# Fused state-space, attention and feed-forward layer: normalized rows turned by DMA, image mask added by VectorE, leaner sine tables

## The chip, the cores and the metric

The kernel runs on one core of one Trainium2 chip. The metric is the device time of one execution in microseconds (us): median 3081.81 us of three runs (3081.46 to 3085.93). The core has TensorE (PE), VectorE (DVE), ScalarE (ACT), GpSimd (POOL) and SyncE (SP, which issues DMAs), and each engine works through its own instructions in order.

## The reference

The program computes three things in a row, for a batch of 32 images.

1. **State-space rows.** `K = einsum('chn,hnl->chl', Wc, exp(P))` with `P = dt*Lambda*pos`: complex exponentials over 1024 positions for 128 rows of each image, of which the real part is kept. The result (32 x 128 x 1024) gets 77 text rows under each image, so `h` is 32 x 205 x 1024.
2. **Attention with a residual.** `x = layernorm(h)`, `q = x @ wq` (32 heads of 32), `k` and `v` with 8 heads, causal mask, softmax, `out @ wo`, `h = h + out`.
3. **A feed-forward product with a residual.** `h = h + layernorm(h) @ W.T + b`, where `W` is a base matrix plus a low-rank update passed through a Fourier matrix.

```
scores = einsum('bihd,bjhd->bhij', q, k) * SCALE
scores = where(tril(ones((s, s))), scores, finfo.min)
attn = softmax(scores, axis=-1)
```

Precision comes from splitting: each fp32 value is written as a high and a low fp16 part, and a product is three fp16 matmuls (high x high, high x low, low x high).

## The kernel before

Five stages follow one another, each a block that all engines leave together.

**State-space tables and product (`ssm`).** The exponential of a position is a product of a coarse and a fine factor. DVE, ACT and POOL first make four tables `tab[:, 0..3]` of 128 x 2048 (two coarse, two fine: a sine and a quarter-turned sine each) and two tables of magnitudes `size`. The argument of a sine is `f*step` (`bases`, L276), plus a phase by ACT (`turned`, L212), less its nearest whole number by DVE (L297, L298); then ACT takes the sine (L223). `size` is a product on POOL (L186) and an exponential on ACT (L216). POOL multiplies two tables by `size` (L191), DVE the other two (L347). Then 16 chunks of 8 channels run: DVE makes `es` from the tables (two instructions at L356, and L358, which adds the two halves for `SUMMED` = 2 channels so that those need one matmul and not two), POOL multiplies the weights (L199, L200), DVE adds (L362), PE multiplies (L379), ACT copies out (L237).

**Weight split (`prep_qkv`).** Untouched by the change.

**Attention.** This is a software pipeline over images that runs through the *rounds* b = -3 to 32 (`steps`). In round b four images are in work: image b gets softmax and `attn @ v` (`has["att"]`), image b+1 its row maxima (`has["max"]`), image b+2 its projections (`has["qkv"]`), image b+3 its layer norm (`has["ln"]`), and image b+4 is loaded. A round has eight *beats* g = 0 to 7 (`SLOTS`), one for each key head. The order inside a beat is written out by hand for each engine:

- PE: `scores` k = 0 and 1 (L867), `score_rows` k = 0 and 1 (the first image rows, L910 and L912, then text rows), the first half (`FRONT`) of the beat's projection `q` (L930 to L932), `scores` k = 2 (L870), `score_rows` k = 2, the second half, then `weigh` of the beat before (L897), then the other *units* of the beat.
- ACT: three exponentials (L720), three casts to fp16 `ph` (L727), then the high part of each unit (L735, or L733 for maxima).
- DVE: row maxima (L805) k = 0 and 1, a unit's low part left from the beat before, maxima k = 2, low part `pl` (L833), a piece of the layer norm in beats 0 to 3 (last piece L786: subtract the mean, multiply by the inverse deviation, 128 x 1024 and 77 x 1024), `norm` (L754 to L760: divide by the softmax sum), then the low part (L813) of every unit of the beat but the last.
- SP: regrouping copies `restack` (L593, 12 DMAs for each half of `q` or `k`), the maxima rows (L640, L641), the load of image b+4 (L644, L645) and the store of a finished image (L649, L650).

A unit is one result in one of the two PSUM buffers `psJ`: `q` 0 to 7 (one a beat), `v` 0 and 1 (beats 0, 1), `k` 0 and 1 (beats 2, 3), `m` 1 (beat 0) and `m` 0 (beat 4), which are the maxima turned to rows, and `x` 0 to 3 (beats 4 to 7), which are the normalized rows of image b+3 turned to columns by PE (L954) for the projections of the next round. PE starts unit number N of a round only when the low parts of the units 0 to N-2 are done (`wait(pe, pj_lo, base + (n + which - 1))` in `project`).

PE also adds the causal mask: in `score_rows` a matmul of an identity by the mask (L910, 128 x 512 for the image rows) starts the sum in PSUM, and the four score matmuls add to it. DVE's maximum over 512 columns then is one instruction for four heads.

**Output weights (`prep_out`) and output stage (`output`).** Untouched. The output stage already turns its fp16 rows with transposing DMAs (L1215, L1217, L1222, L1224).

Of the kernel before, what the change touches and what calls it, by code (L numbers as in the profile page):

```python
# [16 lines left out]
P = 128  # L17
# [17 lines left out]
SUMMED = 2  # L35
HC = 8
MROW = 32768.0
STACK = 3 * HD
# [32 lines left out]
def ssm(nc, x, txt, log_dt, lam, hcat, ahead, peak):  # L71

    NCH = H // HC
    with ExitStack() as ctx:
# [10 lines left out]
        phase = sb("phase", [P, 4])  # L87
# [38 lines left out]
        ab_ok, base_ok, turned_ok, frac_ok, sine_ok = (sem("ab_ok"), sem("base_ok"), sem("turned_ok"),  # L126
                                                       sem("frac_ok"), sem("sine_ok"))
        size_arg, size_ok, tab_cd, tab_ab = sem("size_arg"), sem("size_ok"), sem("tab_cd"), sem("tab_ab")
# [28 lines left out]
        def _(sp):  # L157
# [6 lines left out]
            sp.wait_ge(tab_ab, 2)  # L164
            sp.wait_ge(tab_cd, 2)
# [11 lines left out]
        def _(pool):  # L177
# [6 lines left out]
            pool.wait_ge(ab_ok, 1)  # L184
            for k in range(2):
                pool.tensor_tensor(size[:, k], per_row(a[:]), per_step(iqr[:, k, :]), ALU.mult).then_inc(size_arg, 1)  # L186

            pool.wait_ge(size_ok, 1)
            for t in range(2):
                pool.wait_ge(sine_ok, t + 1)  # L190
                pool.tensor_tensor(tab[:, t], tab[:, t], size[:, 0], ALU.mult).then_inc(tab_ab, 1)  # L191
# [3 lines left out]
            pool.wait_ge(frac_ok, 4)  # L195
# [7 lines left out]
        def _(act):  # L203
            act.wait_ge(in_small, 48)
            act.activation(dt[:], ldt[:], ACT.Exp).then_inc(dt_ok, 1)

            act.wait_ge(args_ok, 1)
            act.activation(ex[:], args[:, 0].rearrange("p k h -> p (k h)"), ACT.Exp).then_inc(waves_ok, 1)
            act.activation(th[:], args[:, 0].rearrange("p k h -> p (k h)"), ACT.Tanh, scale=0.5).then_inc(waves_ok, 1)
            for t in range(4):  # L210
                act.wait_ge(base_ok, t // 2 + 1)
                act.activation(turned[:, t], bases[t // 2], ACT.Identity, bias=phase[:, t:t + 1]).then_inc(turned_ok, 1)  # L212
            act.wait_ge(la_ok, 1)
            act.activation(ela[:], fla[:, 0], ACT.Exp).then_inc(la_exp_ok, 1)
            act.wait_ge(size_arg, 2)
            act.activation(size, size, ACT.Exp).then_inc(size_ok, 1)  # L216

            act.activation(trig[:], turns[:], ACT.Sin, scale=TWO_PI).then_inc(waves_ok, 1)
            act.wait_ge(la_ok, 2)
            act.activation(tla[:], wla[:], ACT.Sin, scale=TWO_PI).then_inc(la_sin_ok, 1)  # L220
            for t in range(4):
                act.wait_ge(frac_ok, t + 1)
                act.activation(tab[:, t], turned[:, t], ACT.Sin, scale=TWO_PI).then_inc(sine_ok, 1)  # L223

            def factors(ch):

                if ch >= 2:
                    act.wait_ge(e_ok, ch - 1)
                act.copy(ab[ch % 2][:], tab[:, 0:2, ch * HC:(ch + 1) * HC, :]).then_inc(ab_in, 1)
# [11 lines left out]
            act.wait_ge(tab_ab, 2)  # L241
# [9 lines left out]
        def _(dve):  # L251
            chain = Chain(dve, dve_c)

            for t, (top, bottom) in enumerate(((0.25, 0.25), (0.5, 0.0), (0.25, 0.0), (0.0, 0.25))):
                dve.memset(phase[0:N, t:t + 1], top)
                m = dve.memset(phase[N:P, t:t + 1], bottom)
# [18 lines left out]
            for k in range(2):  # L275
                dve.tensor_tensor(bases[k], per_row(f[:]), per_step(iqr[:, k, :]), ALU.mult).then_inc(base_ok, 1)  # L276
# [9 lines left out]
            chain(dve.tensor_tensor(turns[:], turns[:], whole[:], ALU.subtract))  # L286

            v = ila[:].unsqueeze(2).broadcast_to([P, LA, H])
            dve.tensor_tensor(fla[:, 0], a[:].unsqueeze(1).broadcast_to([P, LA, H]), v, ALU.mult).then_inc(la_ok, 1)
# [5 lines left out]
            for t in range(4):  # L295
# [155 lines left out]
def attention(nc, ahead, hcat, acat, qh, ql, kh, kl, escale):  # L451
# [5 lines left out]
    with ExitStack() as ctx:  # L457
# [45 lines left out]
        def units(has):  # L503

            out = []
            for s in SLOTS:
# [7 lines left out]
                if s >= 4 and has["ln"]:  # L514
                    row.append(("x", s - 4))
# [906 lines left out]
```

## Time and profile before

| | us |
|---|---|
| median of three runs | 3081.81 |
| the profiled execution | 3082.04 |
| its span, first to last instruction | 3080.3 |
| state-space stage | 0 to 190.7 |
| weight split, then constants | 190.7 to 246.4 |
| attention | 246.4 to about 1895 |
| output weights | about 1895 to 1996 |
| output stage | 1996 to 3080 |

The profile gives each engine's busy time, the granted clock of PE as a share of full speed, groups of instructions with their mean duration, and for idle time the instruction that ended it. The duration of a pipelined instruction is longer than the distance between two of its kind, so durations may overlap in the timeline.

### The profile page before, as it was taken

Reading aid. Unit: us, or ns where it says so; the run is one execution under the profiler, and the core shown is the slowest. Engines: PE = TensorE matmul, PEld = TensorE weight load, DVE = VectorE, ACT = ScalarE, POOL = GpSimd, SP = SyncE. Lnnn points to the kernel's source line nnn. Section 1 sums busy time; section 2 is a strip of 40 time slices with the busy share of each in tenths; the row PEclk is TensorE's granted clock in tenths of the full one; section 3 lists DMA queues with packets and bytes.
Section 4 is the critical chain, followed back from the end, with each engine's and each line's share of the span. In section 5 each row is a group of like instructions: output and inputs, shape, how many; then the busy total and the mean of one; then the engine's idle time right before and its main releaser. Section 6 shows DMA issues by size and latency. Waiting matters only on the chain. (4 is left out here: it accounts for less than half of the span.)

```text
span 3080.3 us, 70678 instructions
## 1 busy us (share of the span) xinstructions
PE 2781.2 (90%) x27970; PEld 2030.8 (66%) x28224; DVE 1997.8 (65%) x4642; ACT 1094.1 (36%) x2362; POOL 1029.9 (33%) x1402
## 2 busy tenths in 40 slices
PE   0847799999999999999999986699999999999999
PEld 0736698989899898989898883244444444444444
DVE  8874577787787878777787865444444444444443
ACT  3331355555555555555555565211001101100110
POOL 4631254544545454554445454011101110110110
PEclk9977899999999999999999996599999999999999
DMA  5642422222222322222222223154554455455453
GB/s 179 194 116 69 103 58 78 58 75 78 57 76 60 80 58 77 69 65 77 56 76 58 69 49 144 55 122 120 129 137 123 121 133 132 118 127 137 124 122 86
DMA packets 446040, 297.32 MB, mean 97 GB/s; under 512 B 389416, under 2 KB 407976, under 8 KB 445232
## 3 DMA queue, kind: packets, MB, share of 16 engines
q1 hardware_dynamic: 445472, 282.69, 35.7%
q10 hardware_dynamic: 240, 10.09, 1.1%
q8 instruction: 226, 3.70, 0.5%
q14 instruction: 102, 0.84, 0.1%
HBM read 116.36 MB, written 80.61 MB: 64 GB/s over the span
## 5 line engine op out<-in xcount | busy, mean ns | idle before, releaser
L693 POOL TENSOR_SCALAR_AFFINE_SELECT p<-p 128x256 f32<-128x256 f32 (+1 forms) x768 | 334.3, 437 | 762.0 <-ACT p L720 743.6
L805 DVE TENSOR_REDUCE mx<-psS 77x2 f32<-77x410 f32 (+1 forms) x768 | 449.3, 613 | 181.9 <-PE psS L912 110.7
L930 PE MATMUL psJ<-xth,qh 128*128 128x205 f16 x2048 | 522.0, 255 | 24.9 <-DVE qsl L813 24.7
L932 PE MATMUL psJ<-xth,ql 128*128 128x205 f16 x2048 | 518.4, 253 | 0.0
L931 PE MATMUL psJ<-xtl,qh 128*128 128x205 f16 x2048 | 516.5, 252 | 0.0
L720 ACT ACTIVATE p<-psT,escale 128x410 f32<-128x410 f32 (+1 forms) x768 | 410.4, 570 | 276.2 <-PE psT L870 256.8
L698 POOL TENSOR_TENSOR pl<-p,ph 128x410 f16<-128x410 f32 (+1 forms) x512 | 447.7, 894 | 102.5 <-ACT ph L727 95.7
L1257 POOL TENSOR_TENSOR hb<-h,bias_sb 128x1024 f32<-128x1024 f32 x52 | 122.5, 2355 | 962.4 <-DVE h L1293 962.4
L1271 ACT CAST xh<-xn 128x1024 f16<-128x1024 f32 x52 | 54.4, 1045 | 967.1 <-DVE xn L1302 967.1
L1332 PE MATMUL ps5O<-woh,ath 128*128 128x512 f16 x832 | 316.2, 380 | 26.3 <-DMA atl<-al 26.3
L1293 DVE SCALAR_TENSOR_TENSOR h<-ps5O,osc,h_in 128x512 f32<-128x512 f32 x104 | 78.1, 751 | 402.4 <-PE ps5O L1334 402.4
L727 ACT CAST ph<-p 128x410 f16<-128x410 f32 (+1 forms) x768 | 334.3, 500 | 6.6 <-POOL p L693 6.4
L1332 PE MATMUL ps5F<-wfh,xth 128*128 128x512 f16 x832 | 315.4, 379 | 1.2 <-DMA xtl<-xl 1.2
L1334 PE MATMUL ps5O<-woh,atl 128*128 128x512 f16 x832 | 316.2, 380 | 0.0
L1333 PE MATMUL ps5O<-wol,ath 128*128 128x512 f16 x832 | 316.2, 380 | 0.0
L1333 PE MATMUL ps5F<-wfl,xth 128*128 128x512 f16 x832 | 315.5, 379 | 0.0
L1334 PE MATMUL ps5F<-wfh,xtl 128*128 128x512 f16 x832 | 315.5, 379 | 0.0
L897 PE MATMUL psO<-vh,ph 128*128 128x33 f16 (+1 forms) x3072 | 261.4, 178 | 6.9 <-issue 5.1
L897 PE MATMUL psO<-vh,pl 128*128 128x33 f16 (+1 forms) x3072 | 260.4, 178 | 0.0
L897 PE MATMUL psO<-vl,ph 128*128 128x33 f16 (+1 forms) x3072 | 260.4, 178 | 0.0
L897 PEld LDWEIGHTS psO<-vh,ph 128*128 128x128 f16 (+1 forms) x3072 | 245.2, 97 | 9.8 <-issue 9.5
L897 PEld LDWEIGHTS psO<-vl,ph 128*128 128x128 f16 (+1 forms) x3072 | 240.7, 97 | 0.0
(227 smaller groups left out, 5906.9 us busy)
## 6 DMA issues: line engine op xcount, KB each, us to landing
a_in<-acat SPq DMA_DIRECT2D x52, 512.0 KB, 3.8
h_in<-hcat SPq DMA_DIRECT2D x52, 512.0 KB, 4.7
qst<-qsh SPq DMA_DIRECT2D x512, 51.2 KB, 2.1
out<-y SPq DMA_DIRECT2D x51, 512.0 KB, 3.1
hcat<-ob SPq DMA_DIRECT2D x64, 256.0 KB, 4.0
xin<-hcat SPq DMA_DIRECT2D x32, 512.0 KB
acat<-ao SPq DMA_DIRECT2D x32, 512.0 KB
qst<-qsl SPq DMA_DIRECT2D x256, 51.2 KB, 2.1
```

What stands on the lines that cost most here:

```text
L693: pool.affine_select(out=v, in_=v, compare_op=ALU.is_ge, fill=0.0, base=0, pattern=[[0, v.shape[1]], [1, w]], channel_multiplier=-1).then_ ...
L698: pool.tensor_tensor(view(pl, g % 2, k), view(p32, g % 2, k), view(ph, g % 2, k), ALU.subtract).then_inc(lo_pool, 1)
L720: act.activation(view(p32, g % 2, k), ps_view(psT[(g + k) % 2], k), ACT.Exp, scale=(escale[:, 0:1] if k < 2 else escale[0:TXT, 0:1])).then ...
L727: act.copy(view(ph, g % 2, k), view(p32, g % 2, k)).then_inc(hi_done, 1)
L805: dve.tensor_reduce(dst, v, AX.X, ALU.max).then_inc(s_read, 1)
L897: m = pe.matmul(o[:, t, r, :], p, v[0:T[j], j, g, :], start=n == 0, stop=n == len(list_) - 1)
L930: pe.matmul(ps[:, 0:S], wh[:, k, c], xth[:, par, k, :], start=k == 0, stop=False)
L931: pe.matmul(ps[:, 0:S], wh[:, k, c], xtl[:, par, k, :], start=False, stop=False)
L932: m = pe.matmul(ps[:, 0:S], wl[:, k, c], xth[:, par, k, :], start=False, stop=k == KC - 1)
L1332: pe.matmul(ps[h][:], th[:, k, :], wh[:, k, c], start=k == 0, stop=False)
L1333: pe.matmul(ps[h][:], th[:, k, :], wl[:, k, c], start=False, stop=False)
L1334: m = pe.matmul(ps[h][:], tl[:, k, :], wh[:, k, c], start=False, stop=k == KC - 1)
```

## The change

Three parts, in `ssm` and `attention`.

**The normalized rows.** The `x` units, L954 and L786 go. DVE makes the negated mean only (`nmean`); ACT, after the units of beats 4 and 5, subtracts the mean in place and casts the scaled row to fp16 (`high_part`); DVE makes the low part after its `pl` of the same beats (`low_part`), and SP turns four pieces with `dma_start_transpose`, the text rows padded to 80. PE waits for them at the start of the next round. The load and the store of an image move from SP to ACT (load and half a store ahead of beat 2, the other half ahead of beat 6), and on SP the first `k` half now goes ahead of the first `q` half. `norm` has one reciprocal and one product instead of two of each.

**The mask.** L910 goes. For the image rows, DVE adds the mask and takes the maximum with one `tensor_tensor_reduce` a head, four where one reduction stood.

**The tables.** ACT makes `size` and `ela` with 36 exponentials of 128 columns, whose scale is the step. Two rounded arguments are made, not four; the quarter-turned sines come from an absolute value. DVE multiplies all four tables by `size`. `SUMMED` goes, and PE makes two matmuls for each channel.

```
+            for k in range(2):
+                for r in range(LR):
+                    m = act.activation(size[:, k, :, r], a[:], ACT.Exp, scale=iqr[:, k, r:r + 1])
+                m.then_inc(size_ok, 1)
...
+            act.activation(turned[:, 1], turned[:, 0], ACT.Abs, scale=-1.0, bias=phase[:, 0:1]).then_inc(far_ok, 1)
+            act.activation(tab[:, 1], turned[:, 0], ACT.Sin, scale=-TWO_PI, bias=lag[:, 0:1]).then_inc(sine_ok, 1)
+            act.wait_ge(far_ok, 1)
+            act.activation(tab[:, 0], turned[:, 1], ACT.Sin, scale=-TWO_PI, bias=quarter[:, 0:1]).then_inc(sine_ok, 1)
...
-            for t in range(4):
-                dve.wait_ge(turned_ok, t + 1)
-                chain(dve.tensor_scalar(tab[:, t], turned[:, t], ROUND, ROUND, ALU.add, ALU.subtract))
-                dve.tensor_tensor(turned[:, t], turned[:, t], tab[:, t], ALU.subtract).then_inc(frac_ok, 1)
+            chain(dve.tensor_scalar(tab[:, 0], base, phase[:, 0:1], ROUND, ALU.add, ALU.add))
+            dve.scalar_tensor_tensor(turned[:, 0], tab[:, 0], ROUND, base, ALU.subtract,
+                                     ALU.subtract).then_inc(frac_ok, 1)
...
+            for t in range(4):
+                dve.tensor_tensor(tab[:, t], tab[:, t], size[:, t // 2], ALU.mult).then_inc(tab_ok, 1)
...
-                if s >= 4 and has["ln"]:
-                    row.append(("x", s - 4))
...
+                if has["ln"]:
+
+                    wait(sp, pj_filled, base)
+                    for t in range(2):
+                        turn(t, nxt, b + 3)
...
+            def turn(t, to, n):
+                r, cols = ((P, slice(0, P)), (TROWS, slice(P, P + TROWS)))[t]
+                sp.wait_ge(x_hi, 2 * n + t + 1)
+                sp.dma_start_transpose(out=xth[:, to, :, cols], in_=xfh[0:r, t, :]).then_inc(xt_in[to], 16)
+                sp.wait_ge(x_lo, 2 * n + t + 1)
+                sp.dma_start_transpose(out=xtl[:, to, :, cols], in_=xfl[0:r, t, :]).then_inc(xt_in[to], 16)
...
+            def high_part(b, par, t):
+                r, x = T[t], xin[0:T[t], 1 - par, t, :]
+                if t == 0:
+                    act.wait_ge(ln_done, b + 4)
...
+                act.activation(x, x, ACT.Identity, bias=nmean[0:r, t:t + 1]).then_inc(centred, 1)
+                act.wait_ge(centred, 2 * (b + 3) + t + 1)
+                act.activation(xfh[0:r, t, :], x, ACT.Copy, scale=rs[0:r, 3, t:t + 1]).then_inc(x_hi, 1)
...
+                    if g == 2 and has["load"]:
+                        wait(act, x_lo, 2 * (b + 3))
+                        load(b + 4, par)
+                    if g == 2 and has["last"]:
+                        store(b - 1, 1)
+                    if g == 6 and has["att"]:
+                        store(b, 0)
...
+                    if g in (4, 5) and has["ln"]:
+                        high_part(b, par, g - 4)
...
+            def low_part(b, par, t):
+                r = T[t]
+                dve.wait_ge(x_hi, 2 * (b + 3) + t + 1)
+                dve.scalar_tensor_tensor(xfl[0:r, t, :], xin[0:r, 1 - par, t, :], rs[0:r, 3, t:t + 1], xfh[0:r, t, :],
+                                         ALU.mult, ALU.subtract).then_inc(x_lo, 1)
...
+                        for r in range(REP):
+                            m = dve.tensor_tensor_reduce(seen[:, r, :], src[:, r * P:(r + 1) * P], mask[:, 0, :], 1.0, LEAST,
+                                                         ALU.add, ALU.max, mx[:, 0, 4 * j + r:4 * j + r + 1])
+                        m.then_inc(s_read, 1)
...
+                    if has["ln"] and g in (4, 5):
+                        low_part(b, par, g - 4)
...
-                    pe.matmul(ps[:], ident_bf[:], mask[:], start=True, stop=False, skip_group_check=True)
...
+                if has["qkv"]:
+                    pe.wait_ge(xt_in[par], 64 * ((b + 2) // 2 + 1))
```

The order of DVE's instructions before, from `pl` of beat 4 to the maxima of beat 5 (`qsl` here is the low part of q4, `xtl` that of unit x0, `ml` that of m0):

```order
L833 TENSOR_TENSOR pl<-p,ph 128x410 [waits hi_done]
L754 RECIPROCAL rden<-psO 128x4 [waits norm_done,av_done]
L755 RECIPROCAL rden<-psO 77x4
L760 TENSOR_TENSOR ao<-psO,rden 128x128 [waits rec_done]
L760 TENSOR_TENSOR ao<-psO,rden 77x128
L813 TENSOR_TENSOR qsl<-psJ,qsh 128x205 [waits pj_hi]
L813 TENSOR_TENSOR xtl<-psJ,xth 128x4x128 [waits pj_hi]
L805 TENSOR_REDUCE mx<-psS 128x4 [waits s_filled]
L805 TENSOR_REDUCE mx<-psS 77x2 [waits s_filled]
```

The same place on DVE now (`xfl` is the low part of the normalized rows; each `tensor_tensor_reduce` stands as two rows named ISA; the first of four pairs is shown):

```order
L865 TENSOR_TENSOR pl<-p,ph 128x410 [waits hi_done]
L814 SCALAR_TENSOR_TENSOR xfl<-xin,rs,xfh 128x1024 [waits x_hi3]
L784 RECIPROCAL rden<-psO 128x8 [waits norm_done,av_done]
L787 TENSOR_TENSOR ao<-psO,rden 128x2x128 [waits rec_done]
L845 TENSOR_TENSOR qsl<-psJ,qsh 128x205 [waits pj_hi]
L831 ISA seen,mx<-psS,mask 128x128 [waits s_filled]
L831 ISA mx 128x1
```

The wait for `x_hi3` now stands ahead of `norm` and of the low part of q4, and the reduction over 512 columns has become eight instructions.

ACT before, from the last cast of beat 4 to the exponentials of beat 6 (`xth` are the high parts of x0 and x1, `mh` that of m0, `p` are the exponentials):

```order
L727 CAST ph<-p 77x308 [waits masked]
L735 CAST qsh<-psJ 128x205 [waits q_in1,pj_filled]
L735 CAST xth<-psJ 128x4x128 [waits pj_filled]
L733 ACTIVATE mh<-psJ 16x205 [waits m_in0,pj_filled]
L720 ACTIVATE p<-psT,escale 128x410 [waits lo_done,st_filled]
L720 ACTIVATE p<-psT,escale 128x410 [waits lo_pool,st_filled]
L720 ACTIVATE p<-psT,escale 77x308 [waits lo_pool,st_filled]
L727 CAST ph<-p 128x410 [waits masked,av_done]
L727 CAST ph<-p 128x410 [waits masked]
```

ACT now, from the last cast of beat 4 to the store ahead of beat 6 (`xfh` is the high part of the normalized rows):

```order
L754 CAST ph<-p 77x308 [waits masked]
L762 CAST qsh<-psJ 128x205 [waits q_in1,pj_filled]
L760 ACTIVATE mh<-psJ 16x205 [waits m_in0,pj_filled]
L719 ACTIVATE xin<-xin,nmean 128x1024 [waits xt_in3_0,ln_done]
L721 ACTIVATE xfh<-xin,rs 128x1024 [waits centred]
L747 ACTIVATE p<-psT,escale 128x410 [waits lo_done,st_filled]
L747 ACTIVATE p<-psT,escale 128x410 [waits lo_pool,st_filled]
L747 ACTIVATE p<-psT,escale 77x308 [waits lo_pool,st_filled]
L754 CAST ph<-p 128x410 [waits masked,av_done]
L754 CAST ph<-p 128x410 [waits masked]
L754 CAST ph<-p 77x308 [waits masked]
L762 CAST qsh<-psJ 128x205 [waits q_in1,pj_filled]
```

After that row the second pair (L719, L721 with 77x1024) follows, then the two DMAs of the store. Where one cast of an `x` unit stood (ahead of `mh` in beat 4), a pair over 1024 columns now stands, behind `mh`.

## Rows read from the trace of the kernel before

**Rows 1.** Windows: stretch, length, busy PE, PEld, DVE, ACT, POOL; clock, DMA share, GB/s.

```profile
0.00:190.70 190.70, 103.31 (x448) 85.73 (x448) 173.09 (x143) 65.93 (x96) 107.89 (x43) 1.00 0.62 180
...
350.00:1843.00 1493.00, 1424.01 (x21098) 1339.61 (x21340) 1171.64 (x3058) 831.65 (x1996) 742.80 (x1215) 1.00 0.26 67
1996.00:3080.00 1084.00, 1079.83 (x4992) 488.66 (x4992) 495.74 (x1142) 101.80 (x102) 122.47 (x52) 1.00 0.50 124
```

**Rows 2.** Line L946 (units m, two a round), 990 to 1100 us.

```profile
L946 PE MATMUL psJ<-ident,mx x5: 272/272/277, 999.0 to 1097.4; 128*16 128x128 f32 x5
```

**Rows 3.** Waits of PE, 1000 to 1600 us: total us, times, longest.

```profile
PE psJ L930 <- DVE qsl L813: 9.5, 12, 0.9
PE psJ L946 <- DVE qsl L813: 7.9, 12, 0.7
```

**Rows 4.** Timeline of PE, beats 4 and 5: start us, us, instruction.

```profile
1026.41 0.51 PE L867 MATMUL psT<-qst,kst 98*128 98x410 f16 x2
...
1027.46 0.25 PE L930 MATMUL psJ<-xth,qh 128*128 128x205 f16 x1
...
1028.53 0.30 PE L870 MATMUL psT<-qst,kst 98*77 98x308 f16 x1
```

**Rows 5.** Timeline of ACT, same place.

```profile
1026.61 0.33 ACT L733 ACTIVATE mh<-psJ 16x205 f16<-16x205 f32 x1 [0.41 <-PE psJ L947]
1026.85 1.06 ACT L720 ACTIVATE p<-psT,escale 128x410 f32<-128x410 f32 x2
1028.86 0.51 ACT L720 ACTIVATE p<-psT,escale 77x308 f32<-77x308 f32 x1 [0.95 <-PE psT L870]
```

**Rows 6.** Timeline of DVE, end of beat 4.

```profile
1025.12 0.18 DVE L754 RECIPROCAL rden<-psO 128x4 f32<-128x4 f32 x1 [0.66 <-PE psO L897]
...
1025.81 0.36 DVE L813 TENSOR_TENSOR qsl<-psJ,qsh 128x205 f16<-128x205 f32 x1
```

**Rows 7.** Groups by shape: count | busy us, mean ns | idle before.

```profile
L805 DVE TENSOR_REDUCE mx<-psS 128x4 f32<-128x512 f32 x256 | 176.2, 688 | 119.4 <-PE psS L912 110.7
...
L760 DVE TENSOR_TENSOR ao<-psO,rden 128x128 f32<-128x128 f32 x256 | 74.8, 292 | 8.8
...
L954 PE MATMUL psJ<-ident,xin 128*128 128x128 f32 x256 | 41.2, 285 | 55.8 <-POOL p L682 55.8
...
L447 DVE SCALAR_TENSOR_TENSOR ql<-stage,qsc,qh 128x1024 f16<-128x1024 f32 x8 | 9.7, 1280 | 0.0
...
L429 ACT ACTIVATE qh<-stage,qsc 128x1024 f16<-128x1024 f32 x8 | 8.4, 1134 | 16.1 <-DVEq L441 16.1
...
L212 ACT ACTIVATE es<-u,phase 128x2048 f32<-128x2048 f32 x4 | 7.7, 1986 | 0.0
```

**Rows 8.** The page, part 6: transposing DMAs of the output stage, us to landing.

```profile
xtl<-xl SPq DMA_TRANSPOSE x52, 2.8
```

**Rows 9.** Windows around two pauses of PE.

```profile
286.40:293.20 6.80, 5.14 (x33) 4.80 (x34) 2.61 (x5) 0.00 (x0) 0.00 (x0) 0.50 0.10 21
...
1487.80:1491.20 3.40, 3.40 (x22) 3.00 (x21) 1.72 (x4) 1.25 (x3) 0.49 (x1) 0.51 0.10 21
```

**Rows 10.** Groups: casts of the attention (L727), then instructions of the state-space tables.

```profile
L727 ACT CAST ph<-p 128x410 f16<-128x410 f32 (+1 forms) x768 | 334.3, 500 | 6.6 <-POOL p L693 6.4
...
L298 DVE TENSOR_TENSOR es<-es,tab 128x2048 f32<-128x2048 f32 x4 | 13.4, 3340 | 0.1
...
L276 DVE TENSOR_TENSOR u<-f,iqr 128x2048 f32<-128x2048 f32 x2 | 7.8, 3962 | 0.0
...
L297 DVE TENSOR_SCALAR tab<-es 128x2048 f32<-128x2048 f32 x4 | 4.9, 1220 | 0.0
...
L301 DVE SCALAR_TENSOR_TENSOR t<-ex,th 128x256 f32<-128x256 f32 x1 | 4.7, 4720 | 0.0
...
L274 DVE TENSOR_SCALAR f<-b 128x128 f32<-128x128 f32 x1 | 3.6, 3610 | 0.0
```

**Rows 11.** Waits of PE in the attention's first rounds, 240 to 400 us.

```profile
PE psT L867 <- DMA qst<-ml: 11.5, 1, 11.5
```

More of the change, by code:

```diff
@@ L183, in _ @@
                       allow_small_or_imprecise_dtypes=True).then_inc(iota_ok, 1)
[L184 to L191, printed above, removed]
             pool.wait_ge(gg_ok, 1)
             pool.wait_ge(in_x, 32)
-            pool.wait_ge(frac_ok, 4)
+            pool.wait_ge(frac_ok, 2)
             for ch in range(NCH):
@@ L205, in _ @@
             act.activation(dt[:], ldt[:], ACT.Exp).then_inc(dt_ok, 1)
+            act.wait_ge(ab_ok, 1)
+            for k in range(2):
+                for r in range(LR):
+                    m = act.activation(size[:, k, :, r], a[:], ACT.Exp, scale=iqr[:, k, r:r + 1])
+                m.then_inc(size_ok, 1)
+            for la in range(LA):
+                m = act.activation(ela[:, la, :], a[:], ACT.Exp, scale=ila[:, la:la + 1])
+            m.then_inc(la_exp_ok, 1)
             act.wait_ge(args_ok, 1)
@@ L252, in _ @@
             chain = Chain(dve, dve_c)
-            for t, (top, bottom) in enumerate(((0.25, 0.25), (0.5, 0.0), (0.25, 0.0), (0.0, 0.25))):
-                dve.memset(phase[0:N, t:t + 1], top)
-                m = dve.memset(phase[N:P, t:t + 1], bottom)
+            for half, back in ((slice(0, N), 0.0), (slice(N, P), -0.25)):
+                dve.memset(phase[half], back)
+                dve.memset(lag[half], back * TWO_PI)
+            m = dve.memset(quarter[:], 0.25 * TWO_PI)
             chain(m)
@@ L376, in _ @@
                         pe.wait_ge(k_read, n - 3)
-                    last = 0 if j < SUMMED else 1
-                    for k in range(last + 1):
+                    for k in range(2):
                         m = pe.matmul(ps[n % 4][:, j % 2, :], u[:, ch % 2, j].rearrange("p a c -> p (a c)"),
-                                      es[:, ch % 2, k, j, :], start=k == 0, stop=k == last)
+                                      es[:, ch % 2, k, j, :], start=k == 0, stop=k == 1)
                     if j % 2:
@@ L613, in step @@
                     shift_rows(1, par)
-                if has["load"]:
-                    wait(sp, pj_filled, base)
-                    load(b + 4, par)
                 if b == -1:
@@ L621, in step @@
                         sp.dma_start(dst, src).then_inc(arrived, 16)
-                if has["last"]:
-                    store(b - 1, nxt)
                 if has["qkv"]:
+                    wait(sp, pj_lo, base + at(rows, "k", 0) + 1)
+                    wait(sp, st_filled, 24 * b + 12)
+                    restack(K_PARTS, kst[par], slice(0, 1), k_in[0])
                     wait(sp, pj_lo, base + at(rows, "q", 3) + 1)
-                    wait(sp, st_filled, 24 * b + 12)
                     restack(Q_PARTS, qst[par], HALVES[0], q_in[0])
@@ L632, in step @@
                     shift_rows(0, nxt)
-                if has["qkv"]:
-                    wait(sp, pj_lo, base + at(rows, "k", 0) + 1)
-                    restack(K_PARTS, kst[par], slice(0, 1), k_in[0])
+                if has["ln"]:
+                    wait(sp, pj_filled, base)
+                    for t in range(2):
+                        turn(t, nxt, b + 3)
             def shift_rows(half, to):
```

159 lines of the change are left out of this document (74 added, 85 removed).

## The prediction

> **What bounds the kernel now.** I read the windows by stage first, then PE's waits inside the longest stage, then the timelines of the three busy engines in one beat. From 350 to 1843 us, inside attention, PE is busy 1424.0 of 1493.0 us (95%), DVE 78%, ACT 56% [rows 1]. Attention therefore runs at PE's pace, and a round takes (1097.4 - 999.0)/2 = 49.2 us [rows 2]. PE's pauses there are short: 0.8 us once a round for the low part of a q, and 0.65 us once a round for unit m0 [rows 3]. The output stage is PE from end to end (1079.83 of 1084.0 us) and nothing in it changes. In the state-space stage DVE is busy 173.09 of 190.7 us [rows 1]. So a gain needs less work on PE in the rounds or on DVE in the tables; a loss needs only one wait of PE that is new.
>
> **What PE loses in a round.** (a) The mask matmul of the image rows, 512 columns, eight a round. In the output stage 4992 matmuls of that width take 1084.0 us, 0.217 each [rows 1]: 1.74 us. (b) The 16 transposes: 41.2/256 = 0.16 us for the wider ones, tails included [rows 7], so at most 2.6 us; tails overlap the next instruction, and I take 1.8. (c) m0's wait for the low part of q4: 7.9/12 = 0.65 us [rows 3]. In its place m0 waits for the low part of k1, made a beat earlier. Together 4.2 us a round.
>
> **Where the layer norm's rows now go.** PE may start q5 only when q4's low part is done. Before, DVE had it at 1025.81 [rows 6], ahead of the beat. Now `low_part` of the image rows stands on DVE ahead of `norm` and of that low part, and it waits for ACT's `high_part`, which ACT reaches behind m0's cast. I count from beat 5's start on PE, 1026.41 [rows 4].
> - ACT casts m0 at +0.20 and is free at +0.44 (1026.61 to 1026.85) [rows 5]; m0 comes directly before the beat's start now as before. Two activations of 1024 columns follow: half of 1986 ns, and 1134 ns [rows 7], with the wait between them 2.2 us. High part at +2.65.
> - DVE: 1.28 for the low part [rows 7], +3.95; `norm`, 0.69 before (1025.12 to 1025.81) [rows 6] and about 0.55 with one reciprocal and one product; q4's low part 0.36. Done at +4.9.
> - PE wanted q5 at 1027.46, +1.05 [rows 4], now +0.83 without the mask. It waits 4.1 us.
>
> Then the same again, one beat on. Half a projection lasts 1.07 us (1027.46 to 1028.53) [rows 4], so `scores` k = 2 comes at +6.0; ACT answers 0.33 later (1028.86) [rows 5], needs that exponential, three casts of 334.3/768 = 0.44 [rows 10], a short wait for POOL's mask and q5's cast, 1.9 in all, +8.2; `high_part` of the text rows (same width, same time) +10.4; DVE's low part +11.7, `norm` +12.25, and then the first maxima of beat 6, 1.15 us: +13.4. Beat 5 would have lasted 4.24 us on PE and lasts 8.35; in beat 6 PE reaches the maxima k = 2, which reuse the PSUM buffer of k = 0, 2.0 us in, at +10.35, and waits 3.1 us. Beats 5 and 6 together lose 7.2 us.
>
> **The other terms of a round.**
> - Load and half a store ahead of ACT's beat 2: four DMA issues. The nearest rows are the ACT instructions they delay; four issues of about 0.4 us (my estimate; between 0, if they pass while ACT still works, and 2.4) push the first exponential to about +2.6, and PE wants its buffer at +1.87: 0.75 us. The half store ahead of beat 6 lies under `high_part`.
> - `tensor_tensor_reduce` isn't in the trace. Four with four accumulator reads replace one reduction of 0.69. A DVE product of 128 columns from PSUM lasts 0.292 us [rows 7]. Bounds for the four: 0.7, what the one reduction takes, and 1.8, four such products and four reads of an estimated 0.16 with no overlap; I take 1.15, four whole products, since successive DVE instructions overlap by about what a read would add. PE needs the first maxima 1.4 us after it filled them, so 1.15 just fits; 1.8 would cost 0.5 in each of eight beats, 4 us a round.
> - Beat 2 also holds DVE's reciprocal square root, behind which q2's low part sits (the 0.8 us wait above); with the longer maxima that wait grows by 0.35.
> - SP: four transposing DMAs at 2.8 us to landing [rows 8], issued from about +8 to +13.5, landed by +17. The next round starts at about +20, so the wait for them is hidden by beat 7, with 3 us to spare.
> - The removed L786, the four low parts of x units and their casts free 5 us of DVE and 2 of ACT, outside the path.
>
> Sum: -4.2 + 7.2 + 0.75 + 0.35 = +4.1 a round, for the 29 rounds 0 to 28 that have both softmax and layer norm: +119.
>
> **The clock.** Behind a pause of PE the granted clock stood at 0.5 (1.2 GHz) once for 6.8 us and once for 3.4 us [rows 9]; over the long stretch of attention it was 1.00 (2.4 GHz) [rows 1]. Half speed over 3.4 us costs 1.7, over 6.8 us 3.4. Now each round has a pause of 4.1 and one of 3.1 us. Bounds 0 and 3.4 a round; I take 1.2: +35. "TensorE: Matmul & The Clock Gate" of the Trainium skill, in the part on the HAM clock gate, says that an idle PE falls back to half rate and must be busy again before it is released, and its practical advice is to leave no long gaps; the two stretches at 0.5 agree. By that rule with a fall in every round the term would be up to 29 x 3.4 = 99 and not 35.
>
> **State-space stage.** DVE's list ahead of the first `es`: L297 and L298 take 4.9 + 13.4 = 18.3 us for four arguments [rows 10]; two are left, and the part of L298 beyond 4 x 2.2 goes, since POOL no longer multiplies beside it: 6.9, so -11.4. L276 at 7.8 and L301 at 4.7 us [rows 10] are long for 2 x 2048 and 256 columns while POOL's L186 and L191 run; without them I estimate 4.4 and 0.4: -7.7. L274 beside L186 likewise, about -3; one product less for `ela`, -0.7; two products of 2.2 more, +4.4. Net -18.4. ACT's 36 exponentials at 0.25 to 0.33 us end near 20 us, under DVE's list, which needs the last sine only at 41. "VectorE: DVE Perf Modes" of the skill, in its section on the TRN2 errata, warns that many small instructions each pay the fixed cost; by it the 36 would cost over 10 us of ACT, still hidden. PE gets four more instructions in each of 16 chunks, 28 so far (448 in 103.31 us, 0.23 each [rows 1]): between 0 and 16 x 0.9 = 15 us; PE isn't what a chunk waits for now, so I take +1. Stage: -17.5 in round numbers.
>
> **Start-up and end.** Before, PE got its first projection input over its own transposes; now ACT, DVE, SP and a landing follow POOL's longer constants: +5. Going into round 0 PE waited 11.5 us for a maxima row [rows 11], whose DMA stands on SP behind the weights' load; the four transposes now stand behind it, and PE waits for them as well: +6. The last three rounds have no layer norm and only lose the mask: -5.
>
> **Sum.** 3082.04 + 119 + 35 - 17.5 + 11 - 5 = 3224.5; the profiled execution lies within 0.3 us of the median of the runs, so 3225.
>
> **Rivals.**
> 1. *The waits in beats 5 and 6 are mostly hidden* (faster). If ACT's and DVE's idle time took in the layer norm pieces, a round would lose 4.2 and gain 1.1 back, -3.1: 3082 - 90 - 17.5 + 11 - 5 = 2981. For it: ACT is idle 44% of attention. Against it: that idle time lies before `scores` k = 2, where ACT waits for PE (0.95 us [rows 5]), and DVE's order puts the wait ahead of what PE needs. It decides at a high part ready by about +0.3, instead of +2.65.
> 2. *`tensor_tensor_reduce` is slow* at 1.8 us or more for four: another 4 us a round, 32 rounds: 3225 + 128 = 3353. For it: eight instructions for one, and each accumulator read may wait for the product ahead of it. Against it: small DVE instructions overlap in these rows.
> 3. *The transposes come late*: if a transposed piece needed 5 us instead of 2.8 behind the other traffic, the next round would start about 3 us later: 3225 + 87 = 3312. Against it: 26% DMA share in attention [rows 1].
> 4. *The clock holds*: 3190, inside my range; *it falls each time*: 3290.
>
> **Chances.** Mine, with 4 in it, 0.68; rival 2 0.10; rival 3 0.07; rival 1 0.09; the rest, 0.06, are halves of the stalls against all savings, around 3050 to 3110. The range from 3110 to 3330 leaves out rival 1 and most of rival 2. Faster by over 0.2% (what a measurement can tell) 0.11, within it 0.02, slower 0.87.
>
> **What would show it.** In the profile after: rounds of 54 to 55 us; PE waiting some 4 us a round at a `q` matmul (L963) for the low part of a q, and some 3 us at a maxima matmul of text rows; DVE waiting for ACT's `xfh` some 5 us a round; stretches at clock 0.5 in attention; the first `es` 18 us earlier. I'm wrong if DVE's wait for `xfh` is under 1 us, or if PE's new waits sit at `scores`, the transposes' landing or the maxima in every beat.

## The result and the profile after

The changed kernel takes 3258.59 us (median of 4 runs, 3244.19 to 3271.26) against 3081.64 us of the kernel before beside it: a ratio of 1.0588, 95% interval 1.0514 to 1.0662. It is slower by 177 us, and the time lies inside the range, 34 us over the predicted one. Further below, one of ten runs of e7_moved_pe_mask (3307.05 us, mean granted clock 0.84) fell in a slower state of the chip, and its ratio leaves that run out. The profiled execution is the longest of the four (3271.26 us, span 3269.5), so the account by rows below is made against it: 3271.3 - 3082.0 = +189.

Windows of the kernel after, columns as in [rows 1]: the state-space stage up to the last chunk, the long part of attention, the output stage.

```profile
0.00:182.00 182.00, 112.48 (x512) 97.69 (x512) 147.76 (x121) 69.38 (x129) 88.97 (x39) 0.99 0.68 195
360.00:1900.00 1540.00, 1313.04 (x18767) 1208.86 (x18765) 1034.99 (x3820) 831.85 (x1813) 707.24 (x1099) 0.93 0.32 75
2190.00:3260.00 1070.00, 1068.80 (x4952) 484.22 (x4951) 494.27 (x1140) 101.78 (x102) 122.50 (x52) 1.00 0.50 124
```

The output stage is unchanged. The first stage is shorter: its last matmul begins at 175.0 us, before at 190.3. In attention PE's busy share falls from 95% to 85%, and its granted clock from 1.00 to 0.93. DVE's share falls too (67%, before 78%), and so does ACT's a little (54%): the engines wait for each other.

How long a round is, by the transpose that begins unit m0 or m1, as in [rows 2]. Seven in a row are three rounds, (1278.4 - 1110.4)/3 = 56.0 us, where it was 49.2:

```profile
L979 PE MATMUL psJ<-ident,mx x7: 269/269/273, 1110.4 to 1278.4; 128*16 128x128 f32 x7
```

Three rounds are a small sample, so here is the whole stretch from m0 of round 0 (the last unit of beat 4) to m0 of round 29, 29 rounds on, in the kernel before and then in the changed one:

```profile
L946 PE MATMUL psJ<-ident,mx x59: 269/273/278, 383.2 to 1817.2; 128*16 128x128 f32 x59
L979 PE MATMUL psJ<-ident,mx x59: 269/269/273, 382.3 to 2003.2; 128*16 128x128 f32 x59
```

The means are 49.45 and 55.89 us a round, which makes 1620.9 - 1434.0 = +187 us. Up to m0 of round 0 the changed kernel is 1 us ahead (382.3 for 383.2), and from m0 of round 29 to the end it takes 3 us longer (1266 for 1263): -1 + 187 + 3 = +189.

PE's waits from 1000 to 1600 us, against [rows 3], and below them DVE's longest in the same stretch:

```profile
PE psJ L963 <- DVE qsl L845: 53.2, 21, 4.0
PE psS L949 <- DVE mx L831: 20.9, 11, 2.0
PE psT L904 <- ACT p L747: 14.8, 21, 1.4
```

```profile
DVE xfl L814 <- ACT xfh L721: 75.4, 22, 3.6
```

Eleven rounds lie in that stretch. In each, PE waits once for 4.0 us at a q matmul and once for about 1.9 at the text rows' maxima, and DVE waits twice, 3.4 to 3.6 us, for ACT's high part. How these hang together is seen in beat 5, which begins at 1110.58. First ACT, from m0's cast on, then DVE, then PE at the matmul that waits:

```profile
1110.78 0.33 ACT L760 ACTIVATE mh<-psJ 16x205 f16<-16x205 f32 x1 [0.45 <-PE psJ L980]
1111.02 1.13 ACT L719 ACTIVATE xin<-xin,nmean 128x1024 f32<-128x1024 f32 x1
1112.18 1.15 ACT L721 ACTIVATE xfh<-xin,rs 128x1024 f16<-128x1024 f32 x1
1113.24 1.08 ACT L747 ACTIVATE p<-psT,escale 128x410 f32<-128x410 f32 x2
```

```profile
1113.37 1.28 DVE L814 SCALAR_TENSOR_TENSOR xfl<-xin,rs,xfh 128x1024 f16<-128x1024 f32 x1 [3.43 <-ACT xfh L721]
1114.57 0.20 DVE L784 RECIPROCAL rden<-psO 128x8 f32<-128x8 f32 x1
1114.81 0.43 DVE L787 TENSOR_TENSOR ao<-psO,rden 128x256 f32<-128x256 f32 x1
1115.15 0.37 DVE L845 TENSOR_TENSOR qsl<-psJ,qsh 128x205 f16<-128x205 f32 x1
```

```profile
1115.57 0.35 PE L963 MATMUL psJ<-xth,qh 128*128 128x205 f16 x1 [4.00 <-DVE qsl L845]
...
1117.60 0.47 PE L904 MATMUL psT<-qst,kst 98*77 98x308 f16 x1
```

The chain is the predicted one: +0.20 the cast, +2.75 the high part (predicted +2.65), +4.07 DVE's low part (+3.95), +4.94 q4's low part (+4.9), PE at +4.99. The reader should see one more thing: the half projection behind the wait lasts 1117.60 - 1115.57 = 2.03 us, where it lasted 1.07 in [rows 4]. The clock has fallen. Two windows, the first behind the pause and the second ahead of it:

```profile
1114.40:1121.10 6.70, 5.53 (x51) 4.96 (x52) 3.76 (x16) 2.18 (x6) 2.92 (x5) 0.50 0.31 65
1066.60:1114.30 47.70, 41.26 (x620) 38.25 (x618) 33.73 (x124) 27.36 (x61) 22.69 (x36) 1.00 0.33 79
```

Such a stretch at half speed (1.2 GHz) comes in each of the 29 rounds behind the 4.0 us pause, 6.8 us long in 25 of them and 3.4 in four, and in 14 rounds another of 3.4 us follows, mostly behind the wait at the maxima. From 380 to 1980 us the profile has 43 of them, 232 us in all; before there was one of 3.4 us up to 1843.

DVE's maxima, for which one reduction of 0.688 us stood in the first line of [rows 7]. The accumulator reads overlap with the products:

```profile
L831 DVE CUSTOM_DVE_ANT_0 seen<-psS,mask 128x128 bf16<-128x128 f32 x1024 | 235.3, 286 | 137.1 <-PE psS L945 136.8
...
L831 DVE DVE_READ_ACCUMULATOR2_ANT mx<- 128x1 f32 x1024 | 84.8, 83 | 0.0
```

In the timeline the four products start 0.21 us apart and the last read ends 0.93 us after the first product began (1106.94 to 1107.87).

### The profile page after: what moved, and what is told of

The parts are those of the page before. It is cut to its first block and busy times, and to the rows that moved or that the text cites. A ratio compares the mean times of both kernels' runs of the same rounds, so it can differ in the third digit from the quotient of the medians.

```text
span 3269.5 us, 70812 instructions
## 1 busy us (share of the span) xinstructions
PE 2806.8 (86%) x27520; PEld 2027.1 (62%) x27520; DVE 1926.4 (59%) x5804; ACT 1185.9 (36%) x2394; POOL 1050.5 (32%) x1400
## 5 line engine op out<-in xcount | busy, mean ns | idle before, releaser
L963 PE MATMUL psJ<-xth,qh 128*128 128x205 f16 x2048 | 552.0, 270 | 215.7 <-DVE qsl L845 148.5
L690 POOL TENSOR_SCALAR_AFFINE_SELECT p<-p 128x256 f32<-128x256 f32 (+1 forms) x768 | 363.7, 479 | 924.5 <-ACT p L747 909.7
L964 PE MATMUL psJ<-xtl,qh 128*128 128x205 f16 x2048 | 551.1, 269 | 0.0
L965 PE MATMUL psJ<-xth,ql 128*128 128x205 f16 x2048 | 550.6, 269 | 0.0
L695 POOL TENSOR_TENSOR pl<-p,ph 128x410 f16<-128x410 f32 (+1 forms) x512 | 458.0, 914 | 101.9 <-ACT ph L754 94.7
L963 PEld LDWEIGHTS psJ<-xth,qh 128*128 128x128 f16 x2048 | 213.0, 104 | 238.4 <-DVE qsl L845 162.3
L837 DVE TENSOR_REDUCE mx<-psS 77x2 f32<-77x410 f32 x512 | 295.6, 577 | 94.3 <-PE psS L952 84.9
L831 DVE CUSTOM_DVE_ANT_0 seen<-psS,mask 128x128 bf16<-128x128 f32 x1024 | 235.3, 286 | 137.1 <-PE psS L945 136.8
```

Source lines behind the costliest of these rows:

```text
L690: pool.affine_select(out=v, in_=v, compare_op=ALU.is_ge, fill=0.0, base=0, pattern=[[0, v.shape[1]], [1, w]], channel_multiplier=-1).then_ ...
L695: pool.tensor_tensor(view(pl, g % 2, k), view(p32, g % 2, k), view(ph, g % 2, k), ALU.subtract).then_inc(lo_pool, 1)
L837: dve.tensor_reduce(dst, v, AX.X, ALU.max).then_inc(s_read, 1)
L963: pe.matmul(ps[:, 0:S], wh[:, k, c], xth[:, par, k, 0:S], start=k == 0, stop=False)
L964: pe.matmul(ps[:, 0:S], wh[:, k, c], xtl[:, par, k, 0:S], start=False, stop=False)
L965: m = pe.matmul(ps[:, 0:S], wl[:, k, c], xth[:, par, k, 0:S], start=False, stop=k == KC - 1)
```

## The experiments

The theory behind the prediction: the loss is the third part of the change, the layer norm's rows, because ACT's and DVE's new work stands ahead of a low part that PE needs in beats 5 and 6, and because the clock falls behind the pause. The rivals: the maxima on VectorE are the loss; PE's waits are there for other reasons than the place of this work; the clock costs little.

### One part at a time

**e1_tables_only**: the kernel before with the new state-space function `ssm` and nothing else.

> The kernel before with the new state-space tables alone. In the changed kernel DVE's first es stands at 57.3 us instead of 70.75, so theory: faster by 13 to 14 us, about 3068, all of it before the attention starts. Rival (the tables' gain is given back by the 64 added matmul passes of the chunks): within 3 us of before.

3063.39 us (3062.49 to 3065.5), ratio 0.9940, interval 0.9925 to 0.9955: -17 us. The tables are a gain by themselves; it is 3 to 4 us more than expected here. The trace places 13.8 us of it ahead of m0 of round 0 (369.4 us, before 383.2); most of the rest is in the rounds, which e1 runs without a clock fall.

**e2_mask_only**: the kernel before with VectorE's masked maxima of the image rows and without the mask matmul; the rows of the layer norm and the tables stay.

```
-  pe.matmul(ps[:], ident_bf[:], mask[:], start=True, stop=False, ...)
+  m = dve.tensor_tensor_reduce(seen[:, r, :], src[:, r*P:(r+1)*P], mask[:, 0, :], ...)
```

> The kernel before with the image rows' mask added by DVE alone, PE's mask matmul gone. Theory (PE is the bound of a round and loses 1.74 us; DVE's four instructions take 0.92 us in the changed kernel instead of 0.60, which lengthens one wait of PE a round by 0.3): a round of 47.8 us instead of 49.2, total about 3037. Rival (DVE's longer maxima hold PE in every beat): 3080 or more.

3065.62 us (3057.2 to 3068.81), ratio 0.9942, interval 0.9921 to 0.9962: -15 us, a third of what I expected. A regular round lasts 48.25 to 48.4 us, 0.9 less than before. Two things take the rest. PE's wait for q's low part grows from 0.73 to 0.95 us, since DVE's maxima are 0.24 us longer than the reduction and stand ahead of it (the profile's waits from 1000 to 1600 us, as in [rows 3]):

```profile
PE psJ L937 <- DVE qsl L821: 12.9, 13, 1.1
PE psJ L953 <- DVE qsl L821: 7.9, 12, 0.7
PE psS L919 <- issue: 5.0, 6, 2.1
```

And without its waits the round has lost some 1.1 us and not 8 x 0.217 = 1.74. By beats (medians of PE's beats, waits taken off), beats 2, 3, 5 and 6 are 0.21 to 0.23 us shorter, a full matmul, but beats 4 and 7 only 0.05. Why those give less isn't shown. The third line is a wait at the first maxima for which this profile names no releaser; in the kernel before the same matmul waits five times, 3.6 us in all, for restacked K rows from SP's DMAs. Behind such a pause the clock fell three times in this run.

**e3_rows_only**: the changed kernel with the mask matmul and the old `ssm` put back, so that only the layer norm's rows differ from the kernel before.

> The changed kernel with the old tables and PE's mask again, so before plus the transposing DMAs with the layer norm's pieces on ACT and DVE. Theory (these cause the whole loss, the other two parts gain 13 and 45 us): about 3315 to 3330. Rival (the loss comes from the parts together, DVE's longer maxima behind the waits): under 3270.

3286.76 us (3259.43 to 3289.03), ratio 1.0643, interval 1.0599 to 1.0687: +206 us, 30 to 45 under my figure, which had put the mask's gain at 45 us. The third part is the whole loss, and the parts add up: -17 - 15 + 206 = +174, measured +177. That refutes the rival that blames the maxima.

### The clock by itself

**e5_warm**: the changed kernel, with matmuls whose result nobody reads where PE would wait: 36 of 248 columns ahead of q5 and 18 ahead of the last maxima of beat 6.

```
+  def idle_work(b, g, count):
+      wait(pe, norm_done, 8 * b + g - 2)
+      for _ in range(count):
+          pe.matmul(spare[(g - 1) % 2], qh[:, 0, 0:P], qh[:, 1, 0:248], ...)
```

> The changed kernel with matmuls that nobody reads, put where PE waits: 36 of 248 columns (3.8 us at full clock) ahead of q5's matmuls in beat 5, 18 (1.9 us) ahead of the last maxima of beat 6, in the 29 rounds with a layer norm; the results are untouched. Theory (the fall of the granted clock to half behind the 4 us wait costs some 3 us a round by itself): the clock stays at 1.00 in attention, a round of about 53 us, total about 3180. Rival (the clock costs nothing because PE has time to spare behind the wait): 3255 or more.

3193.24 us (3191.66 to 3195.45), ratio 1.0372, interval 1.0356 to 1.0387. The window over attention:

```profile
362.00:1900.00 1538.00, 1457.85 (x21257) 1354.15 (x21256) 1085.51 (x4010) 872.64 (x1903) 742.23 (x1154) 1.00 0.35 79
```

The clock is 1.00, and most rounds last 53.1 to 53.5 us. The 29 rounds, measured as above:

```profile
L981 PE MATMUL psJ<-ident,mx x59: 269/269/273, 381.8 to 1928.0; 128*16 128x128 f32 x59
```

This is the round without the clock's share: 1546.2/29 = 53.3 on the mean, 53.3 - 49.4 = +3.9 (predicted +4.1); beat 5 lasts 8.41 us (predicted 8.35). The clock costs the rest, 55.9 - 53.3 = 2.6 us a round, 65 us in the medians of the runs. It may be 0.3 more, since the 18 matmuls overfill their gap: beat 6 lasts 7.25 us here and 6.9 in the changed kernel. 54 superfluous matmuls a round make the kernel faster by 2%.

### Where ACT's and DVE's work should stand

**e4_low_late**: in the changed kernel DVE makes the two low parts in beats 5 and 6 instead of 4 and 5.

> The changed kernel with DVE's low part of the normalized rows moved by one beat (beats 5 and 6 instead of 4 and 5), nothing else. Theory A (the loss is DVE's place in the order: its wait for ACT stands ahead of norm and of the low part that PE needs): PE's 4.0 us wait at the q matmul and the 2 us wait at the maxima go, waits of about 1.4 us for ACT's exponentials stay in two beats, the clock mostly holds; a round of 49 to 50 us, total about 3085. Theory B (ACT's added 4.5 us in beats 4 and 5 sets the loss wherever DVE waits): a round of 54 us or more, total above 3220.

3135.96 us (3116.69 to 3141.19), ratio 1.0153, interval 1.0116 to 1.0191. One beat later, and 123 us of 177 are gone. The 4.0 us wait has become these (1000 to 1600 us):

```profile
PE psT L904 <- ACT p L747: 32.0, 35, 1.5
PE psT L901 <- DMA xtl<-xfl: 15.9, 9, 3.1
PE psJ L963 <- DVE qsl L845: 10.2, 11, 1.0
PE psS L949 <- DVE mx L831: 9.0, 12, 0.8
```

Two are new: in beat 5 ACT's high part now holds up its own exponentials (1.04 us), and the turned rows come late for the next round (1.6 us in the median). The clock stays at 1.00 in most rounds. It is 50 us over my expectation, which had waits for the exponentials but none for the turned rows.

**e6_moved**: ACT centres and casts the image rows in beat 3, centres the text rows in beat 4 and casts them in beat 5, each behind a q's cast; load and half store go behind q2's cast; DVE's low parts are in beats 4 and 6; PE waits for the turned rows right ahead of q0's matmuls and not at the round's start.

```
+  def between(b, par, has, g):        # called behind the cast of a q
+      ...
+      if has["ln"] and g in (3, 4):
+          centre(b, par, g - 3)
+      if has["ln"] and g in (3, 5):
+          high_part(b, par, (g - 3) // 2)
```

> The changed kernel with the layer norm's pieces in places where their engines stood idle: ACT subtracts the mean and casts the image rows between q3's and k1's casts of beat 3, subtracts the text rows' mean behind q4's cast and casts them behind q5's, load and store stand behind q2's cast; DVE's low parts in beats 4 and 6; PE waits for the turned rows ahead of q0's matmuls only. Theory A (the loss is where the waits stand, not the amount of work): rounds of 45 to 46 us, total 2960 to 2985. Theory B (the transposes on the DMA queue or the added ACT and DVE work cost a round in any place): 3060 or more.

3071.43 us (3056.26 to 3084.93, 10 runs), ratio 0.9985, interval 0.9959 to 1.0011: no difference from before. The rows' loss is gone, but the 90 to 110 us that I had expected below before aren't there. **e7_moved_pe_mask** is the same with the mask matmul:

> The same as the moved kernel but with PE's mask matmul and one DVE reduction again. Theory: PE bound, so 1.74 us a round longer less what DVE's shorter maxima give back, 45 to 55 us slower than the moved kernel, about 3020. Rival (with PE's work gone DVE is the bound, so the mask on DVE costs): faster than the moved kernel.

3086.48 us (10 runs, nine of them 3060.33 to 3094.12), ratio 1.0020, interval 0.9997 to 1.0043. By the medians the mask is worth some 15 us here too, as in e2, though the two intervals overlap; I had expected 45 to 55. The traces show where it went: with PE's mask matmul back, PE's four waits of a round are 3.1 us together, and 4.3 without it. PE's waits in e6, 1000 to 1600 us:

```profile
PE psJ L974 <- DVE qsl L856: 25.3, 24, 1.2
PE psJ L974 <- DMA xtl<-xfl: 16.1, 12, 3.0
PE psS L960 <- DVE mx L842: 10.3, 12, 0.9
```

These are 0.88 and 1.23 us for a q's low part in beats 3 and 5, 0.86 for the maxima in beat 7, and 1.3 on the mean for the turned rows at q0: 4.3 us a round. So the median round is 48.9 us with all savings in it.

**e8_moved2**: `nmean` already in beat 1, both of ACT's centrings behind q2's cast, both casts behind q3's, load and store behind q1's, DVE's low parts last in beats 4 and 5. **e9_moved2_low_ahead** differs from it only in DVE's low parts, which stand ahead of `norm` and of q's low part, as in the changed kernel.

> The layer norm's pieces earlier than in the moved kernel: DVE negates the mean in beat 1; ACT subtracts it from both parts behind q2's cast (beat 2) and casts both behind q3's (beat 3), where it waited 2.4 us for a k unit; load and store stand behind q1's cast; DVE's low parts come last in beats 4 and 5, behind norm and the low part of q. Theory A (what was left in the moved kernel is three waits a round: 1.2 us at the q matmuls of beat 5, 0.85 at the maxima of beat 7, 1.3 for late transposes in beat 0): all three go, a round of 45.5 to 46.5 us, total 2975 to 3005. Theory B (a round cannot be much under 48.5 us, since DVE or the DMA queue is the bound): within 15 us of the moved kernel's 3071.

> As the kernel above, but with DVE's low parts ahead of norm and of q's low part, where the changed kernel has them; their input is ready a beat before, so DVE never waits for it. Theory A (the place on DVE alone costs what q's low part comes later, 1.28 us less DVE's idle 0.7): 0.5 to 1.2 us of PE's wait in beat 5, total 15 to 35 us over the kernel above, still under 3035. Rival (the place on DVE is what cost the changed kernel 4 us in beat 5, whenever the input is ready): over 3150.

e8: 3094.61 us (12 runs), ratio 1.0045, interval 1.0023 to 1.0066. e9: 3091.19 us (6 runs), ratio 1.0048, interval 1.0026 to 1.0070. Both expectations missed: e8 is slower than before, and e9 is no slower than e8. In e8, rounds with a full clock last 48.3 to 49.4 us, but 18 rounds have a clock fall of 3.4 us. All 18 stand behind the wait for the turned rows at q0 where that wait was 1.5 to 2.9 us; of the rounds without a fall all but one had 0.8 to 1.6 us there. So it is once more the turned rows that cost. Between e8 and e9 there is nothing. That is the useful part: a low part ahead of q's low part costs PE a wait of 1.23 us in beat 5 when its input is ready, and 4.0 us in the changed kernel. What made most of the loss was the wait for ACT that the low part brought with it, not its own 1.28 us of DVE. In both, the turned rows stayed late at q0 although their low parts were made earlier. That pointed to the queue that turns them.

### SP's list

SP in e6 around the end of a round (start, duration of issuing): no gap from the restacking of k to here.

```profile
1026.03 0.59 SPq L640 DMA_DIRECT2D qst<-ml  x1
1026.72 1.25 SPq L645 DMA_TRANSPOSE xth<-xfh  x1
1028.02 1.31 SPq L647 DMA_TRANSPOSE xtl<-xfl  x1
1029.38 1.28 SPq L645 DMA_TRANSPOSE xth<-xfh  x1
1030.70 2.34 SPq L647 DMA_TRANSPOSE xtl<-xfl  x1
1033.14 2.44 SPq L595 DMA_DIRECT2D kst<-ksh  x4
```

The input of the last transpose was ready by then: DVE's low part of the text rows began at 1026.0 and took 2.03 us, and the DMA that turns it was issued at 1030.70.

**e11_moved_turn_ahead**: e6, with the four transposes issued ahead of the two small DMAs of the row maxima (`shift_rows(0, nxt)`).

> As the first kernel with moved rows (3071), but SP issues the four transposing DMAs ahead of the two small DMAs of the row maxima instead of behind them. Theory A: at the start of each round TensorE's 0.9 to 1.5 us for the turned low parts is the end of SP's list, which is busy from the restacking of k to here; the two small issues are 1.3 us of it, so the last transpose lands 1.3 us earlier and the wait falls to 0 to 0.3: 29 rounds by about 1.1 = 32 us, 3040; and no new wait at m0. Rival B: the transposes wait for their data or for the DMA engines and not for SP's list: the wait stays at 0.9 or more, 3065 to 3075. Rival C: the row maxima then come late at the next round's first scores, and PE waits there about 1 us for qst: 3070 or more.

3145.48 us (3131.97 to 3150.69), ratio 1.0209, interval 1.0181 to 1.0237: 74 us over e6, the third case and far beyond the 1 us a round that I had put on it.

```profile
PE psT L912 <- DMA qst<-ml: 26.2, 12, 3.0
PE psJ L974 <- DVE qsl L856: 24.7, 23, 1.2
PE psS L960 <- DVE mx L842: 10.2, 12, 0.9
```

The wait for the turned rows is gone, and in its place the next round's first scores wait for the row maxima, 2.2 us on the mean and 3.0 at most in this stretch, with a clock fall behind it in almost every round (26 falls from 360 to 1800 us, 7 in e6). In both orders, what stands last on SP is late.

**e12_moved_short_list**: e6 with SP's order as it was, but from round 4 on SP leaves out the third part of k's restacking, 8 DMAs a round.

```
     for k, src in enumerate(parts_):
+        if skip and k == 2:
+            sp.sem_inc(arrived, 64)
+            continue
```

> As the first kernel with moved rows (3071, SP's order as there), but from round 4 on SP leaves out the third of the three parts of k's restacking (4 DMAs of each half, 8 a round, 2.5 us of issuing ahead of the transposes), so that old rows stay in that part of K. It takes SP's list away without moving anything else. Theory A: SP's list is what is late, here and in the kernel with the transposes ahead. The last transpose is then issued when its low part is ready, 2.5 us earlier; TensorE's wait for the turned rows (0.9 to 1.5 us a round) goes, and with it the clock falls behind it: rounds 47.5 to 47.9 instead of 48.9, 25 rounds by 1.1 and some 10 us of clock, 3030 (3015 to 3045). Rival: the transposes wait for their data or for the DMA engines: the wait stays at 0.9 us or more and the time within 10 us of 3071.

3031.46 us (3026.61 to 3035.56), ratio 0.9851, interval 0.9825 to 0.9877: 40 us under e6, at the theory's number.

```profile
PE psJ L977 <- DVE qsl L859: 28.3, 26, 1.2
PE psS L963 <- DVE mx L845: 11.1, 13, 0.9
PE psJ L977 <- DMA xtl<-xfl: 0.5, 1, 0.5
```

The wait for the turned rows is down from 16.1 to 0.5 us, all others stand, and most rounds last 47.5 to 47.7 us. The transposes themselves didn't land sooner (a median of 2.8 us from issue to landing in e6, 2.9 for `xtl` and 3.3 for `xth` here), they were issued sooner. So it is SP's list: it issues at about 0.62 us for each of 48 restacking DMAs, and 5 to 6 us of transposes are more than its slack.

### The version that beats both

**e10_tables_mask**: the kernel before with the tables and VectorE's mask, and TensorE's transposes kept.

> The kernel before with two parts of the change and not the third: the new state-space tables and VectorE's causal mask; the rows of the layer norm are still turned by TensorE. Theory A: the two gains stand in different stages and add up: 3081 - 17 (tables alone) - 15 (mask alone) = 3049, range 3040 to 3060; rounds 48.3 us as in the kernel with the mask alone, first `es` 13 us earlier than before. Rival: the mask's gain was mostly a matter of which rounds lose the clock, and here it is under 5: over 3060.

3046.37 us (3038.85 to 3055.3), ratio 0.9899, interval 0.9874 to 0.9924: -33 us, the sum of the two parts; beside e1 (3063.39) the mask is worth 17 us, so the rival falls. It leaves no work out, and is the fastest of the kernels that leave none out. A regular round lasts 48.3 us, with 2.0 us waits at the first maxima now and then, as in e2.

## Why the prediction was right, step by step

Against the profiled execution (+189, predicted +142.5) the four terms came out like this:

| | predicted | measured |
|---|---|---|
| 29 rounds, clock held | +119 | +112 (e5 against before) |
| clock | +35 | +75 (after against e5) |
| tables and start-up, to m0 of round 0 | -6.5 | -1 |
| behind m0 of round 29 | -5 | +3 |

The mechanism of the loss is the predicted one. Most of what the total is off comes from the clock term, which was half of the measured one; of the rest, part cancels.

- *What PE loses*, 4.2 us a round: 3.8 by PE's beats (medians of before against e5, new waits taken off). The mask is some 1.1 and not 1.74 (e2), m0's wait of 0.65 is gone as predicted, and the transposes with their tails are left with about 2.0 where 1.8 was taken. The latter is by difference and wasn't run alone.
- *Beats 5 and 6*, +7.2: beat 5 is 8.41 us with the clock held (predicted 8.35), beat 6 of the changed kernel's round shown above is 6.87, where the clock is back at 1.00, of which 1.87 are the wait at the maxima and 0.40 one at `scores` (predicted 3.1 at the maxima). Against 4.24 each that is +6.8.
- *ACT's DMA issues* in beat 2, +0.75: PE waits 0.66 to 1.39 at L904 there, 1.04 in the median. *Beat 3*: 0.88 at L963, where 0.73 was before; the growth of 0.35 is mostly not there, since the maxima take 0.93 and not 1.15 us.
- *SP's transposes hidden by beat 7*: right for this kernel, since the loss in beats 5 and 6 itself gives SP 6 us more. It isn't a property of the change: at rounds of 48.9 us they are late (e6). My count of 3 us to spare had only the transposes in it, and neither the full list ahead of them nor an issue of 2.3 us at the end.
- *The clock* is the mis-sized term: 1.2 us a round taken, 2.6 measured (e5 against the profile after), 29 x 1.4 = 40 us of the 47 that the profiled execution lies over the prediction. The other terms miss by -7, +6 and +8. I gave a fall in each round a case of its own (3290) and didn't take it, although [rows 9] show a fall behind each of the two pauses. "TensorE: Matmul & The Clock Gate" of the Trainium skill, in the part on the HAM clock gate, advises against long gaps on PE; the trace agrees (0.50 behind each 4.0 us pause), and its rule with a fall each round gave up to 99 us, of which 75 came.
- *Tables* -17.5: -17 (e1), of which 13.8 are ahead of m0 of round 0, so the match is in part luck. The first `es` comes 13.5 us earlier and not 18 (57.3 us, before 70.75): DVE's four products at L351 take 15.9 us, the first 2.29 and the others 4.6 each, where each product was estimated at 2.2. POOL multiplies beside them, and the prediction had priced them as if it stood idle.
- *Start-up* +11: about +13, since m0 of round 0 begins at 382.3 us and with the new tables alone at 369.4. Round 0 itself begins 21 us later than in e1 (344.3, 323.2), and 8 of them come back in its first five beats. *The last rounds*, -5: not there, +3 from m0 of round 29 to the end. The cause of that stays open.
- *Rival 1*, waits hidden, 2981: moving the work (e6, e8, e9) ends at 3071 to 3095. The pieces find only places where PE waits another 0.9 to 1.2 us, and SP has no room. *Rival 2*: refuted, 0.93 us and not 1.8. *Rival 3*: from round 1 on no transpose is waited for in the changed kernel (ahead of round 0 PE waits 13.9 us for one).
- *The signs*: rounds of 55.9 us (54 to 55 predicted), 4.0 us at L963 as said, 1.9 at the text rows' maxima (some 3), and DVE waiting 6.9 us a round for `xfh` (some 5).

Left open: whether the layer norm's rows could pay with the complete restacking, on another engine's queue; that wasn't tried. That the wait of up to 2.0 us at the first maxima in e2 and e10 is one for restacked K rows is read from the kernel before; their own traces name nothing that ended it.

## What to carry to other kernels

Before moving work off the bottleneck engine, follow each moved piece to what stands behind it on its new engine: an instruction that waits for a third engine costs its wait. Here PE waited 4.0 us where DVE's low part had to wait for ACT (3.4 us), and 1.23 us where it hadn't. Price a recurring pause of TensorE with its clock: if the trace shows a fall behind a pause of that length, take one for each, and test it with idle matmuls. Count the issues of a DMA queue like an engine's busy time; here the last entry was late in both orders tried, and a shorter list helped.

## What the runs showed of the hardware

- `tensor_tensor_reduce` of 128x128 from PSUM is two instructions, 0.286 and 0.083 us, which overlap so that four pairs take 0.93 us.
- A pause of 4.0 us once a round brought a fall to half clock in each of 29 rounds, 6.8 us long in 25 and 3.4 in four. Pauses of 1.2 to 3.5 us ahead of a round's first scores (e11) brought one in nearly every round, mostly of 3.4 us. In e8 waits of 1.5 to 2.9 us at q0 brought 18, and six waits of 0.8 to 1.3 us there none.
- DMA_TRANSPOSE between SBUF tiles held SP for 1.25 to 1.3 us in the median and now and then for over 2; it landed 2.8 to 3.6 us after issue in the median and up to 6.0 (e6, changed kernel).
- A float32 product of 128x2048 on DVE took 2.28 us while POOL stood idle (L294). With POOL's products beside it, three of four at L351 took 4.6 us and one 2.29, and POOL's own took 4.6 instead of the later 2.53.
